# Centring the down weights during attention, and a last norm with squares alone

## What is computed

```python
x = x + _layernorm(_L0_attn_ref(_layernorm(x), w_qkv, w_o, qn_g, qn_b, kn_g, kn_b))
x = x + _layernorm(_L0_ffn_ref(_layernorm(x), gate_w, w_gate, w_up, w_down, shgate_w, shw_gate, shw_up, shw_down))

def _layernorm(x, axis=-1, eps=1e-05):
    m = jnp.mean(x, axis=axis, keepdims=True)
    v = jnp.var(x, axis=axis, keepdims=True)
    return (x - m) / jnp.sqrt(v + eps)

# feed-forward part, for tokens xf (2048 x 256)
logits = einsum('td,ed->te', xf, gate_w); weights, indices = top_k(softmax(logits), 2)   # 8 experts
combine = weights / weights.sum(-1), spread over the 8 experts
h = silu(einsum('td,edh->teh', xf, w_gate)) * einsum('td,edh->teh', xf, w_up)            # h: 176
out = einsum('teh,ehd,te->td', h, w_down, combine)
sh = silu(xf @ shw_gate) * (xf @ shw_up) @ shw_down                                      # 352
out = out + sigmoid(xf @ shgate_w)[:, None] * sh
```

## Time and profile before

| | |
|---|---|
| median of 3 runs | 674.17 us (672.75 to 674.7) |
| the profiled execution | 673.56 us, its span 671.8 us |
| PE busy | 631.1 us, 94% of the span, 4506 matmuls |
| DVE, ACT, POOL busy | 549.9 us (82%), 551.3 us (82%), 530.5 us (79%) |
| attention | some 470 us of the span |
| DMA | 54.27 MB, 81 GB/s in the mean |

### The profile page before, as it was taken

One profiled execution on the slowest core, in us unless ns is written; L12 is line 12 of the kernel. 1 busy time (PEld: TensorE's weight loads), 2 busy tenths in 40 slices (PEclk: granted clock), 3 DMA queues, 4 the chain that ended last, 5 costly groups with the idle time before them and its releaser, 6 DMA issues.

```text
span 671.8 us, 15617 instructions
## 1 busy us (share of the span) xinstructions
PE 631.1 (94%) x4506; PEld 586.9 (87%) x4506; DVE 549.9 (82%) x1912; ACT 551.3 (82%) x2105; POOL 530.5 (79%) x601
## 2 busy tenths in 40 slices
PE   5879999999999999999999999999789989999993
PEld 5657899999999999999999999999678889999991
DVE  3989999898898889899898999979878755555466
ACT  3589999999999999999999999999787536666633
POOL 3698898999899899989989998999757424666664
PEclk9999999999999999999999999999899999999997
DMA  8001306997740000000000000000526033444173
GB/s 328 33 0 33 104 1 198 335 335 209 4 47 1 1 1 1 1 1 2 1 1 1 1 1 2 1 1 25 160 101 229 33 90 111 128 130 119 67 265 125
DMA packets 51122, 54.27 MB, mean 81 GB/s; under 512 B 19840, under 2 KB 42752, under 8 KB 50912
## 3 DMA queue, kind: packets, MB, share of 16 engines
q1 hardware_dynamic: 47632, 43.90, 23.6%
q0 software_dynamic: 3408, 9.38, 3.7%
HBM read 23.83 MB, written 29.51 MB: 79 GB/s over the span
## 4 chain that ended last, share of the span: by engine, by line
PE 75%; DVE 9%; POOL 5%; issue 4%; ACT 4%; DMA 2%; POOLq 0%; SPq 0%; ACTq 0%; DVEq 0%
PE pQ L470 8%; PE pQ L471 8%; PE pQ L472 8%; PE pPO L576 5%; PE pPO L470 5%; PE pPO L472 5%; PE pPO L471 5%; PE pT L548 4%; PE pSS L470 3%; PE pA L470 3%; PE pA L471 3%; PE pA L472 3%; PE pSS L471 2%; PE pSS L472 2%; POOL xs L2076 2%
## 5 line engine op out<-in xcount | busy, mean ns | idle before, releaser
L1002 ACT ACTIVATE P<-P,nmx 128x128 f32<-128x128 f32 (+1 forms) x256 | 118.8, 491 | 1.0 <-DVE nmx L1445 1.0
L470 PE MATMUL pQ<-W 128*128 128x512 f32 (+2 forms) x334 | 116.1, 347 | 2.4 <-DVE W L1359 1.2
L471 PE MATMUL pQ<-W 128*128 128x512 f32 (+2 forms) x334 | 111.6, 334 | 0.0
L472 PE MATMUL pQ<-W 128*128 128x512 f32 (+2 forms) x334 | 111.3, 333 | 0.0
L1982 POOL TENSOR_TENSOR ropes<-ropes 128x640 f32<-128x640 f32 x63 | 99.3, 1576 | 13.7 <-DVE ropes L1422 13.4
L1010 ACT ACTIVATE P<-P,rinv 128x128 f32<-128x128 f32 (+1 forms) x256 | 105.8, 481 | 2.1 <-DVE rinv L1451 2.1
L1992 POOL TENSOR_TENSOR ropes<-ropes 128x640 f32<-128x640 f32 x63 | 99.6, 1580 | 4.9
L470 PE MATMUL pPO<-W 128*128 128x256 f32 (+1 forms) x323 | 95.3, 295 | 5.6 <-DVE W L1460 3.9
L987 ACT ACTIVATE ropes<-pQ 128x128 f32<-128x128 f32 x320 | 88.4, 303 | 9.7 <-PE pQ L472 9.7
L471 PE MATMUL pPO<-W 128*128 128x256 f32 (+1 forms) x323 | 92.0, 285 | 0.0
L472 PE MATMUL pPO<-W 128*128 128x256 f32 (+1 forms) x323 | 91.8, 284 | 0.0
(11 more groups left out here) (272 smaller groups left out, 2170.5 us busy)
## 6 DMA issues: line engine op xcount, KB each, us to landing
xs<-stage SPq DMA_DIRECT2D x1, 17550.0 KB, 58.4
stage<-xs SPq DMA_DIRECT2D x39, 130.0 KB
ropes<-in_ew SPq DMA_DIRECT2D x8, 608.0 KB
stage<-in_wqkv SPq DMA_DIRECT2D x3, 768.0 KB, 9.0
stage<-ys SPq DMA_DIRECT2D x4, 512.0 KB, 7.3
ropes<-ys SPq DMA_DIRECT2D x4, 512.0 KB, 6.8
out<-X SPq DMA_DIRECT2D x7, 256.0 KB, 2.0
X<-in_wo SPq DMA_DIRECT2D x1, 1536.0 KB, 12.7
```

Of the source, the lines that this page charges most:

```text
L470: e.matmul(out, lh, rh, start=start, stop=False, skip_group_check=True)
L471: e.matmul(out, lh, rl, start=False, stop=False, skip_group_check=True)
L472: return e.matmul(out, ll, rh, start=False, stop=stop, skip_group_check=True)
L1002: a = e.activation(P[:, z, span(t)], P[:, z, span(t)], ACT.Exp, bias=nmx[:, z, t:t + 1], scale=-1.0, accum_out=sums[:, z, t:t + 1])
```

## The change

The down weights of the experts and of the shared expert get their mean over the 256 outputs removed, on the chip, in ten chunks (`DOWN`): one for each expert (128 x 512) and two for the shared one (512 and 256 columns). SP loads a chunk into one of two new buffers, DVE sums its rows (`down_mean`, steps 46, 54, ... 118) and subtracts the means (`down_centre`, steps 48, 56, ... 120), and SP stores it into a new tensor `downs` in HBM. The chain stands in SP's list between the `spare` loads and the shared gate and up weights. The down weights are afterwards loaded from `downs`, so the load of an expert becomes two DMAs.

With that the last norm needs no mean. ACT squares the rows of a pair and sums them (`last_square`), POOL makes the root from the sum (`last_root`, two steps in place of four), and DVE multiplies and adds to x in one instruction per tile (`last_add`). `last_stats`, `last_scale`, `last_add_tile` and `last_apply` are gone.

```diff
+DOWN = [(x, EA, EH) for x in range(NE)] + [(NE, 0, 2 * HID), (NE, 2 * HID, NKT * HID)]
+DOWN_SUM = {46 + 8 * c: c for c in range(len(DOWN))}
+DOWN_SUB = {48 + 8 * c: c for c in range(len(DOWN))}
...
+        down_raw = [part(ropes, 2304 + 512 * z, 512) for z in range(2)]
...
+            def load_down(c):
+                x, a, b = DOWN[c]
+                src = ew_d[:, x * EH + a:x * EH + b] if x < NE else sw_d[:, 2 * SHUP + a:2 * SHUP + b]
+                e.dma_start(down_raw[c % 2][:, 0:b - a], src).then_inc(s_ddown, 16)
+
+            load_down(0)
+            for c in range(len(DOWN)):
+                x, a, b = DOWN[c]
+                e.wait_ge(s_down, 2 * c + 1)
+                if c > 0:
+                    e.wait_ge(s_sdown, 16 * c)
+                if c + 1 < len(DOWN):
+                    load_down(c + 1)
+                e.wait_ge(s_down, 2 * c + 2)
+                e.dma_start(downs_d[:, c * 512:c * 512 + b - a], down_raw[c % 2][:, 0:b - a]).then_inc(s_sdown, 16)
             e.dma_start(part(stage, UB, 2 * SHUP), sw_d[:, 0:2 * SHUP]).then_inc(s_dsw, 16)
             e.wait_ge(s_swlo, 2)
-            e.dma_start(sw_raw[2], sw_d[:, 2 * SHUP:]).then_inc(s_dsw, 16)
+            e.wait_ge(s_sdown, 16 * len(DOWN))
+            e.dma_start(sw_raw[2], downs_d[:, NE * 2 * HID:]).then_inc(s_dsw, 16)
...
-                e.dma_start(ew_raw[x % 3], ew_d[:, x * EH:(x + 1) * EH]).then_inc(s_dew[x % 2], 16)
+                e.dma_start(ew_raw[x % 3][:, 0:EA], ew_d[:, x * EH:x * EH + EA]).then_inc(s_dew[x % 2], 16)
+                e.dma_start(ew_raw[x % 3][:, EA:EH], downs_d[:, x * 512:x * 512 + 512]).then_inc(s_dew[x % 2], 16)
...
-            def last_apply(p):
-                e.wait_ge(s_nb2, NB + root_of(p) + 1)
+            def last_square(p):
+                if p < PPE:
+                    e.wait_ge(s_fsum, p + 1)
+                else:
+                    e.wait_ge(s_psum, p - PPE + 1)
+                if p < 4:
+                    e.wait_ge(s_nb2, NB)
+                else:
+                    e.wait_ge(s_lr2, NB + root_of(p - 4) + 1)
                 for t in range(2):
-                    a = e.activation(yl[p][:, t, 0:HID], pair_row[p][:, t, :], ACT.Identity, bias=nb2[:, p % 4, t:t + 1],
-                                     scale=lr2[:, p % 4, t:t + 1])
-                a.then_inc(s_fapp, 1)
+                    a = e.activation(yl[p][:, t, HID:2 * HID], pair_row[p][:, t, :], ACT.Square,
+                                     accum_out=mv2[:, p % 4, t, 1:2])
+                a.then_inc(s_ssq, 1)
...
-                p = PAIR.get(q - 1, 0)
-                if 0 < p < 6 and p % 2 == 1:
-                    last_apply(p - 1)
-                    last_apply(p)
-                elif p == 6:
-                    last_apply(p)
+                if q in PAIR:
+                    last_square(PAIR[q])
...
+            def down_mean(c):
+                rows_c, n = down_rows(c)
+                e.wait_ge(s_ddown, 16 * (c + 1))
+                e.tensor_reduce(down_sum[:, c, 0:n], rows_c, AXX, ALU.add).then_inc(s_down, 1)
+
+            def down_centre(c):
+                rows_c, n = down_rows(c)
+                e.wait_ge(s_down, 2 * c + 1)
+                e.scalar_tensor_tensor(rows_c, down_sum[:, c, 0:n].unsqueeze(2).to_broadcast([128, n, HID]), -1.0 / HID,
+                                       rows_c, ALU.mult, ALU.add).then_inc(s_down, 1)
...
-            def last_stats(p):
...
+            def last_add(p):
                 e.wait_ge(s_lr2, NB + root_of(p) + 1)
                 for t in range(2):
...
+                    x = X[:, 2 * p + t, :]
+                    a = e.scalar_tensor_tensor(x, pair_row[p][:, t, :], lr2[:, p % 4, t:t + 1], x, ALU.mult, ALU.add)
+                    if t == 1 or p == NPAIR - 1:
+                        a.then_inc(s_fres, 1)
...
+                if s in DOWN_SUM:
+                    down_mean(DOWN_SUM[s])
+                if s in DOWN_SUB:
+                    down_centre(DOWN_SUB[s])
...
             def last_root(p, n):
...
-                e.wait_ge(s_aggr2, NB + p + n)
-                e.tensor_scalar(lr2[:, z, :], mv2[:, z, :, 1], 1.0, EPS, ALU.mult, ALU.add).then_inc(s_var2, 1)
-                if p < NPAIR - 1:
-                    e.tensor_scalar(nb2[:, z, :], mv2[:, z, :, 0], -1.0, None, ALU.mult)
+                e.wait_ge(s_ssq, p + n)
+                e.tensor_scalar(lr2[:, z, :], mv2[:, z, :, 1], 1.0 / HID, EPS, ALU.mult, ALU.add).then_inc(s_var2, 1)
```

More of the change, by code:

```diff
@@ L319, in program @@
                              "s_rhi"))
-        s_shared, s_y, s_fapp = (sem(n) for n in ("s_shared", "s_y", "s_fapp"))
+        s_shared, s_y, s_ssq = (sem(n) for n in ("s_shared", "s_y", "s_ssq"))
         s_bn, s_aggr, s_hrow, s_hT, s_wqlo, s_tab_d, s_rope_d = (
@@ L1713, in last_sum @@
                                 ALU.add).then_inc(s_fsum, 1)
-                e.wait_ge(s_fsum, p + 1)
-            def last_stats(p):
-                if p >= PPE:
-                    e.wait_ge(s_psum, p - PPE + 1)
-                    e.wait_ge(s_aggr2, NB + p)
-                for t in range(2):
-                    a = e.bn_stats(st2[:, t, :], pair_row[p][:, t, :])
-                a.then_inc(s_bn2, 1)
-                norm_aggr(NB + p)
-            def last_scale(p):
+            def last_add(p):
                 e.wait_ge(s_lr2, NB + root_of(p) + 1)
                 for t in range(2):
-                    a = e.tensor_scalar(yl[p][:, t, 0:HID], pair_row[p][:, t, :], mv2[:, p % 4, t, 0:1],
-                                        lr2[:, p % 4, t:t + 1], ALU.subtract, ALU.mult)
-                a.then_inc(s_fapp, 1)
-            def last_add_tile(p, t):
-                e.wait_ge(s_fapp, p + 1)
-                e.tensor_tensor(X[:, 2 * p + t, :], X[:, 2 * p + t, :], yl[p][:, t, 0:HID],
-                                ALU.add).then_inc(s_fres, 1)
-            def last_add(p):
-                e.wait_ge(s_fapp, p + 1)
-                e.tensor_tensor(X[:, 2 * p:2 * p + 2, :], X[:, 2 * p:2 * p + 2, :], yl[p][:, :, 0:HID],
-                                ALU.add).then_inc(s_fres, 1)
+                    x = X[:, 2 * p + t, :]
+                    a = e.scalar_tensor_tensor(x, pair_row[p][:, t, :], lr2[:, p % 4, t:t + 1], x, ALU.mult, ALU.add)
+                    if t == 1 or p == NPAIR - 1:
+                        a.then_inc(s_fres, 1)
             def ffn(q):
@@ L1766, in ffn @@
                     last_add(p)
-                elif p == 6:
+                elif p >= 6:
                     last_add(p)
-                elif p == 7:
-                    last_scale(p)
-                    for t in range(2):
-                        last_add_tile(p, t)
             ln1_stats(0)
```

20 lines of the change are left out of this document (10 added, 10 removed).

## The result

The changed kernel takes 705.12 us (median of 6 runs, 703.82 to 707.35) against 674.43 (6 runs) for the kernel before: a ratio of **1.046** (95%: 1.044 to 1.049), 30.7 us slower. The forecast was 696.4 with a range of 688 to 704, so it had the sign and the places, but the time lies outside the range, 8.7 us above the forecast. The profiled execution took 704.04, its span is 702.2.

A forecast was written before the change was run, and what follows sets the result against it. TensorE was taken to set the pace, without a gap in mid-attention. 14.9 + 1.3 + 6.0 + 1.3 + 2.0 - 3.3 = +22.2 us on 673.56, with the runs' median 0.6 higher, gave 696.4 us, range 688 to 704.

The forecast's parts named there:

- Place 1: VectorE at step 46 waits for the first chunk's load, landing at 191.0; TensorE idles 14.9 us (bounds 13.4 and 18.2).
- The clock: TensorE returns from an idle gap at 1.2 GHz: 1.3 us lost after each of the two waits.
- Place 2: ScalarE at step 120 waits for the shared weights, now loaded behind the chunks; TensorE idles 6.0 us, plus 1.3 for clock.
- the rival that it is hidden: The step 120 wait doesn't show, by a quick landing or TensorE's work in hand: 689 us, chance 0.11.
- Place 3: Nine more chunks on VectorE, each a mean and a centring, cost 0.22 us each: 2.0 us (bounds 0 and 4.8).
- The rival of GpSimd's lock: Each centring is held for GpSimd's whole row, 0.6 us in each of nine chunks, 5.4 in all: 701.8 us, chance 0.12.
- Place 4: The last norm behind TensorE's last matmuls gets shorter: a gain of 3.3 us, not above 3.6.
- Slack: TensorE has hidden slack and the loop makes up the waits later: 673 us or below, or 685.5; chance 0.07.
- The rival that the end gains nothing: The last norm gains nothing, since ScalarE has eight pairs of Squares in a row: 699.7 us, chance 0.08.

The follow-up runs named there:

- e5: The changed kernel with the first chunk's load issued ahead of the 4-byte writes and the shared gate and up weights loaded early: 674.5 us, ratio 0.9994.
- e4: The changed kernel with the first chunk's load cut into 32 KB and 224 KB, the first mean taken of 64 columns: 699.3 us in one run, 1.044.
- e12: The changed kernel with the first chunk's load issued by ScalarE at step 46, not by SyncE: 684.1 us in one run, ratio 1.024.
- e1: The changed kernel with the shared gate and up weights loaded early, near step 54, not behind the last store: 691.6 us, ratio 1.033.
- e2: The changed kernel with the means at steps 54, 61, 68 ... 110, 118 and the centrings two steps behind each: 678.7 us, ratio 1.014.
- e9: The changed kernel with the first chunk's load issued by ScalarE at step 43, not by SyncE: 683.5 us in one run, ratio 1.013.
- e10: As e5, but the ninth chunk is the one of 256 columns and stands at steps 104 and 106: 668.1 us, ratio 0.994.
- e6: The changed kernel with the gate and up weights loaded early and the means at steps 56, 60 ... 92: 675.7 us, ratio 1.001.
- e7: The kernel before with the new last norm alone, no chunk loaded, centred or stored: 672.1 us, ratio 0.9957.
- e8: The kernel before, unedited, profiled once more; SyncE's issuing of the 4-byte writes took 21.33 us.

## Why the prediction was right and where it was wrong

The sum was +22.2; the profile shows +30.5 in the time (704.04 against 673.56).

- **Place 1, 16.2 predicted, 23.0 found. This is the step that failed.** The mechanism was right: VectorE waits for the load, TensorE stops with it, and e5 takes it away whole. Its landing was mis-sized, and that in the sentence "so I let it land at 191.0". I added up bytes from the earlier trace rows as if 256 KB were through once 276 KB had flowed. Those rows were of a load of 704 KB, and e4 shows that size hardly counts: 32 KB take 9.3 us to land, 256 KB 10.3, and 704 KB took 11.4. Nor had those bytes arrived. The stretch view counts a packet where it starts, whichever transfer it is of, and of the 704 KB only 132 had ended by 191.0. Taken from the earlier trace rows with size left aside, which is the upper bound that I gave (18.2), the landing misses by 0.7 us. I also took SyncE's 182.87 as fixed. The issue came at 184.73, and the writes ahead of it, which no edit touched, took anything from 17.6 to 22.1 us in fourteen profiles. TensorE's gap is 19.7 us, 4.8 more than the 14.9 of the sum: 2.1 from issue to landing (10.3 for 8.1), 1.9 from the later issue, and 0.8 because TensorE stood there earlier in this profile (at 176.6 for 177.45). Only the first is the byte count's; the other two vary from execution to execution.
- **The clock, 1.3 predicted.** At the first place the marks at step 49 part by 21.7, of which 19.7 are the gap: 2.0 us, "twice as much" being what I had left open. The lower level lasted from before TensorE's return at 196.3 to about 200.3. In e12 a gap of 4.5 us cost 2.7 more. In four gaps the cost beyond their length was close to half of the time at 0.50 behind TensorE's return: 4.1 us after the gap of 19.7 (2.0 lost), 5.6 after that of 4.5 in e12 (2.7 lost for 2.8), 5.9 after that of 6.6 at place 2 (2.7 lost for 2.9), 3.3 after that of 6.7 in e4 (1.5). A longer gap was not followed by a longer stretch at 0.50.
- **A term that I hadn't: 1.1 to 1.3 us at step 57.** The second centring, in step 56, took 2.02 us, the longest: after the pause it falls on a 640-element row of GpSimd, as it does not in e5, which has no pause (0.69). e1, e4 and e12, which pause too, lose 1.1 to 1.3 there, e5 nothing. The place fits; no run moved this centring alone.
- **Place 2, 7.3 predicted, 9.3 found.** ScalarE waited 6.5 (6.8), TensorE 6.6 (6.0), so the wait was sized well, and the rival that it is hidden is out. The rest, 2.7 and not 1.3, falls in the stretch at the half clock from 470 to 480. By the whole time e1 prices it at 8.8. In e2, e4, e9 and e12, which have the same wait, the marks part there by 7.7 to 8.3, as the stretch at 0.50 is shorter.
- **Place 3, 2.0 predicted, 2.3 found, but not as I had it.** I spread it at 0.22 over nine chunks. The first of the nine is the one at step 56, counted above. Seven cost nothing that stays, and the one at steps 110 and 112 costs 2.3, by way of other instructions. That it is this chunk is shown by e10, where it is moved and the 2.3 are gone; that it is by way of those rows is read from the profiles. The reading of the earlier trace rows was of little use: what decided here was less how much VectorE had in hand than what ran on GpSimd when a two-operand row came.
- **The rival of GpSimd's lock** was right in kind and wrong in its place. A held row does its work once GpSimd's has ended, as the Trainium skill has it for two-input rows ("SBUF — State Buffer", Who interferes with whom), and e6 pays 4.5 us for it. But the trace does not bear out the whole rule: the centring at 289.70 was not held by the power row of 5 elements beside it, though both of its inputs and those of GpSimd's row are in SBUF. In the changed kernel seven of the ten centrings began beside such a row and clear of the 640-element rows (0.68 or 0.69 us), and so the rival's +5.4 didn't come. I had asked only whether the new rows would be held, and not which old rows they would push into it.
- **Place 4, -3.3 predicted, -3.7 found up to the last row, -2.6 at the end of the span.** The reading by rows held: the squares, the root and the fused rows took 3.9 from the start of TensorE's last matmuls, for 7.7. That is a little above the 3.6 that I had called the most. What I hadn't is the 1.2 us behind the last row. The rival that the end gains nothing is out by e7.
- **Slack**, the rival on the other side: none. The 23.0 at step 57 are 23.0 at step 109. (ScalarE's 96.38% leave 0.12 us a step and not the 0.14 of my sum, which changes nothing.)
- **The range.** My own bounds with the lock, 18.2, 7.5 and 7.4 for the chunks, 2.6 for the clock, less 3.3, give +32.4 and 706.6 for the median. I cut that to 704 as unlikely together, and the measured 705.12 lies between the two.

With 19.7, 2.0 and 1.3 at place 1, 2.3 at place 3, 9.3 at place 2, -1.4 for the clock at step 131 and -3.7, it is +29.5. The remaining 1.0 are start-up (-1.0), late stretches (+0.8) and what lies behind the last row (+1.2). The first two are within what profiles differ by in stretches that no edit touched: start-up by -1.4 to +0.9, and e8 by 0.7 in the late stretches.

**Still open**: why the 4-byte writes take from 17.6 to 22.1 us, what held the last updates of e12's load, why the gap before step 131 costs the clock in eleven profiles and not in three, why one row of GpSimd holds a centring and another doesn't, and why the program's end takes 1.2 us more in every changed kernel.

## What to carry to other kernels

Behind the tiny writes of this kernel a load landed about when they had drained, whether it had 32 or 704 KB (8.4 to 11.4 us). So take a load's landing from one that stood at the same place, not from bytes, and put it ahead of such writes; another queue helped only in part. A row with two operands in SBUF on VectorE cost here its own 0.7 us or up to 2.0 beside a long row of GpSimd, by where it came, so look at which rows GpSimd runs beside it and beside the short rows that it pushes back. And a change can be good in itself and lose by its place: the same work is 4.6% slower at its first placing, and 0.3 to 0.6% faster with two loads and the ninth chunk moved, a part of the 0.6 being the clock.

## What I had not expected of the hardware

- Behind the 4-byte writes 32 KB land after 9.3 us and 256 KB after 8.4 to 11.1; in quiet stretches 256 KB land after 2.7. The first packet of such a load starts 4.6 to 7.0 us after its issue.
- From another engine's queue 256 KB get in among the writes, and still take 8.5 us for 2.7 to 4.6.
- A row of 80 elements on VectorE takes 1.60 us for 0.23 beside a GpSimd row of 640 elements (1.69 us). One of 512 elements takes its 0.69 beside a GpSimd row of 5 elements (1.17 us).
- The same transfers, in the same kernel, keep SyncE issuing for 17.55 or 21.33 us.
- TensorE's granted clock stays at 0.50 for some 4 us after it returns from a gap of 19.7 us (1.2 GHz, the lower level); after 2.81 us it was 0.50 for some 3 us in the kernel before, and full throughout in three of fourteen profiles.
